# Attention with the row of maxima subtracted once per step, in quarters of the TensorE array

## The reference

```
q = einsum('bnsd,neod->bneso', sx, wq);  k = einsum(... wk);  v = einsum(... wv)
causal = where(tril(ones((s, s))), 0, -inf)
scores = einsum('bnesd,bntd->bnest', q, k) * d ** 0.5 + causal
att = softmax(scores, axis=-1)
qkv = einsum('bnest,bntd->bnesd', att, v)
```

## Time and profile before

| | us |
|---|---|
| median of 3 runs | 3643.19 (3640.71 to 3644.28) |
| profiled execution | 3640.48 |
| its span | 3638.5 |
| TensorE busy | 3115.9 (86%) |
| GpSimd busy | 1863.7 (51%) |
| VectorE busy | 1758.2 (48%) |
| ScalarE busy | 1237.5 (34%) |

### The profile page before, as it was taken

One profiled execution on the slowest core, in us unless ns is written; L12 is line 12 of the kernel. 1 busy time (PEld: TensorE's weight loads), 2 busy tenths in 40 slices (PEclk: granted clock), 3 DMA queues, 4 the chain that ended last, 5 costly groups with the idle time before them and its releaser, 6 DMA issues. The chain is left out here.

```text
span 3638.5 us, 46094 instructions
## 1 busy us (share of the span) xinstructions
PE 3115.9 (86%) x18162; PEld 1885.5 (52%) x18162; DVE 1758.2 (48%) x2797; ACT 1237.5 (34%) x1637; POOL 1863.7 (51%) x992
## 2 busy tenths in 40 slices
PE   7998654775999879899999999969899999999943
PEld 3446333554888545555555555445555555545422
DVE  4512433337774435555555564035555555564046
ACT  2200211015554223343444434423334443434423
POOL 0000000113332025677878889935677878889934
PEclk9999887687999969999999999969999999999967
DMA  9951001009998000000000000000000000000001
GB/s 393 424 172 36 0 0 51 1 8 273 273 280 151 6 14 1 1 1 1 1 1 1 1 1 1 1 1 1 1 1 1 1 1 1 1 1 1 1 4 38
DMA packets 63748, 195.36 MB, mean 54 GB/s; under 512 B 8243, under 2 KB 25137, under 8 KB 53554
## 3 DMA queue, kind: packets, MB, share of 16 engines
q1 hardware_dynamic: 38786, 148.11, 10.5%
q0 software_dynamic: 24752, 44.31, 6.8%
HBM read 188.99 MB, written 3.41 MB: 53 GB/s over the span
## 5 line engine op out<-in xcount | busy, mean ns | idle before, releaser
L1829 POOL TENSOR_TENSOR at_acc<-at_acc,at_pt 128x1024 f32<-128x1024 f32 (+3 forms) x728 | 1557.7, 2140 | 277.0 <-ACT at_pt L1665 193.7
L1725 DVE TENSOR_REDUCE at_mx<-at_psR 128x2 f32<-128x1024 f32 (+3 forms) x784 | 858.8, 1112 | 854.9 <-PE at_psR L1556 540.3
L1665 ACT ACTIVATE at_pt<-at_psR 128x1024 f32<-128x1024 f32 (+3 forms) x784 | 732.0, 936 | 993.3 <-PE at_psR L1577 601.5
L1593 PE MATMUL at_psO<-at_pt,v 128*64 128x512 f32 (+3 forms) x3136 | 706.4, 571 | 16.3 <-DVE at_oT L1744 10.6
L1574 PE MATMUL at_psR<-at_qhi,at_klo 64*128 64x512 f32 (+3 forms) x1568 | 345.5, 435 | 59.2 <-ACT at_pt L1665 28.0
L1556 PE MATMUL at_psR<-at_khi,at_qhi 64*128 64x512 f32 (+3 forms) x1568 | 340.8, 428 | 34.3 <-ACT at_pt L1665 10.2
L1593 PEld LDWEIGHTS at_psO<-at_pt,v 128*64 128x64 f32 x3136 | 193.7, 139 | 339.1 <-issue 275.2
L1209 PE MATMUL ga_acc<-h,ga_ring 128*128 128x257 f32 (+1 forms) x1352 | 307.4, 388 | 28.2 <-ACT ga_ring L1113 24.5
L1574 PEld LDWEIGHTS at_psR<-at_qhi,at_klo 64*128 64x128 f32 x1568 | 152.0, 187 | 331.1 <-issue 307.1
L1574 PE MATMUL at_psR<-at_qlo,at_khi 64*128 64x512 f32 (+3 forms) x1568 | 300.4, 376 | 0.0
L1577 PE MATMUL at_psR<-at_nm,at_ones_r 64*128 64x512 f32 (+3 forms) x1568 | 299.5, 374 | 0.0
(11 more groups left out here) (315 smaller groups left out, 3325.1 us busy)
## 6 DMA issues: line engine op xcount, KB each, us to landing
gc_rows<-in_adj SPq DMA_DIRECT2D x26, 1664.0 KB, 17.4
ga_rows<-in_adj SPq DMA_DIRECT2D x26, 1664.0 KB, 9.9
ga_ring<-in_adjT POOLq DMA_DIRECT2D x78, 512.0 KB, 24.1
gc_cols<-in_adjT SPq DMA_DIRECT2D x26, 1024.0 KB, 14.9
gc_ring<-in_adjT SPq DMA_DIRECT2D x26, 512.0 KB, 7.6
gc_ring<-in_adjT SPq DMA_DIRECT2D x13, 256.0 KB, 2.8
ga_ring<-in_adjT POOLq DMA_DIRECT2D x13, 256.0 KB, 9.9
out_x<-X SPq DMA_DIRECT2D x6, 512.0 KB
```

The source lines that it names most:

```text
L1593: ins = pe.matmul(psO[lanes[l], off:off + w], v1[:, t, (2 * hp + l) * D:(2 * hp + l + 1) * D], pt[:, g % PTS, l, 0:w], start=g == FIRST[u] ...
L1665: act.activation(pt[:, g % PTS, :, 0:w], psR[:, slot_of["score", g] % SLOTS, :, 0:w], ACT.Exp).then_inc(e_ready, 1)
L1725: dve.tensor_reduce(mx[:, u % 2, :, s, c:c + 1].rearrange("p l o -> p (l o)"), psR[:, slot_of["max", i] % SLOTS, :, 0:w], AX.X, ALU.max).t ...
L1829: pool.tensor_tensor(to, to, got, ALU.add).then_inc(added, 1)
```

## The change

The row of maxima is no longer added in `scores`, group by group. A new function `less_maxima` adds it for both groups of a step and both heads before either group's scores: four products, each in a quarter of the array (32 rows), each into a bank of its own. They now begin the accumulation (start=True), and `scores` only adds to it. For that `nm` needs the maxima in four rows, 0, 32, 64 and 96: VectorE writes each maximum twice, the transposes are 97 wide instead of 65, and `negm` has one buffer instead of two, with the wait changed to fit. `less_maxima` takes the slots of both groups; so `slot_users` lists the two score groups of a step first and all the products for maxima after them. The order in which TensorE makes these products changes a little too: the first one stands between the two groups, the others behind the second.

```diff
+QUAD = 32
 def slot_users():
             g = FIRST[u] + 2 * k
+            out += [("score", x) for x in (g + 2, g + 3) if x < FIRST[NU]]
             for half in range(2):
-                if g + 2 + half < FIRST[NU]:
-                    out.append(("score", g + 2 + half))
                 out += [("max", piece[0]) for piece in max_pieces(u, k, half)]
...
-        negm = m.sb("at_negm", [P, 2, SUB, D + 1])
+        negm = m.sb("at_negm", [P, SUB, 3 * QUAD + 1])
+        quads = [[slice((2 * l + i) * QUAD, (2 * l + i + 1) * QUAD) for l in range(2)] for i in range(2)]
...
+                def less_maxima(g):
+                    u = GROUPS[g][0]
+                    pe.wait_ge(x_read, turn_of["r", u] + 1)
+                    slots = [take_slot(pe, ("score", g + i)) for i in range(2)]
+                    for i in range(2):
+                        _, t, off, w = GROUPS[g + i]
+                        for l in range(2):
+                            pe.matmul(psR[:, slots[i], l, 0:w], ones_r[quads[i][l], :],
+                                      nm[quads[i][l], u % 2, off:off + w], start=True, stop=False)
+
                 def scores(g):
-                    pe.wait_ge(x_read, turn_of["r", u] + 1)
-                    slot = take_slot(pe, ("score", g))
+                    slot = slot_of["score", g] % SLOTS
-                    for left, right, first in ((klo, qhi, True), (khi, qlo, False), (khi, qhi, False)):
+                    for left, right, last in ((klo, qhi, False), (khi, qlo, False), (khi, qhi, True)):
                         for l in range(2):
-                            pe.matmul(psR[:, slot, l, 0:w], left[lanes[l], kc:kc + P],
-                                      right[lanes[l], u % 3, off:off + w], start=first, stop=False)
-                    for l in range(2):
-                        ins = pe.matmul(psR[:, slot, l, 0:w], ones_r[lanes[l], :], nm[lanes[l], u % 2, off:off + w],
-                                        start=False, stop=not diag)
+                            ins = pe.matmul(psR[:, slot, l, 0:w], left[lanes[l], kc:kc + P],
+                                            right[lanes[l], u % 3, off:off + w], start=False, stop=last and not diag)
...
-                        for half in range(2):
-                            if g + 2 < ng:
-                                scores(g + 2 + half)
-                            for piece in max_pieces(u, k, half):
-                                row_max(u + 2, *piece)
+                        if g + 2 < ng:
+                            less_maxima(g + 2)
+                        pieces = max_pieces(u, k, 0) + max_pieces(u, k, 1)
+                        if g + 2 < ng:
+                            scores(g + 2)
+                        for piece in pieces[:1]:
+                            row_max(u + 2, *piece)
+                        if g + 2 < ng:
+                            scores(g + 3)
+                        for piece in pieces[1:]:
+                            row_max(u + 2, *piece)
...
                 def maxima(u):
-                    if u >= 2:
-                        dve.wait_ge(x_full, turn_of["r", u - 2] + 1)
+                    if u >= 1:
+                        dve.wait_ge(x_full, turn_of["r", u - 1] + 1)
                     for s in range(bw // P):
-                        ins = dve.tensor_reduce(negm[:, u % 2, s, 0:D + 1:D], mx[:, u % 2, :, s, 0:seen], AX.X, ALU.max, negate=True)
+                        ins = dve.tensor_reduce(negm[:, s, 0:3 * QUAD + 1:QUAD].rearrange("p (l i) -> p l i", i=2),
+                                                mx[:, u % 2, :, s, 0:seen].unsqueeze(2).broadcast_to([P, 2, 2, seen]),
+                                                AX.X, ALU.max, negate=True)
```

More of the change, by code:

```diff
@@ L1528, in row_of_maxima @@
                     for s in range(QBLOCKS[UNITS[u][1]][1] // P):
-                        ins = pe.transpose(psX[0:D + 1, s * P:(s + 1) * P], negm[:, u % 2, s, :], ident[:, :])
+                        ins = pe.transpose(psX[0:3 * QUAD + 1, s * P:(s + 1) * P], negm[:, s, :], ident[:, :])
                     ins.then_inc(x_full, 1)
@@ L1608, in _ @@
                 queries(2)
+                less_maxima(0)
                 scores(0)
@@ L1644, in row_of_maxima @@
                     act.wait_ge(x_full, turn_of["r", u] + 1)
-                    act.activation(nm[0:D + 1, u % 2, 0:bw], psX[0:D + 1, 0:bw], ACT.Copy).then_inc(x_read, 1)
+                    act.activation(nm[0:3 * QUAD + 1, u % 2, 0:bw], psX[0:3 * QUAD + 1, 0:bw], ACT.Copy).then_inc(x_read, 1)
                 def turn_out(u, h):
@@ L1837, in gate @@
                             2).broadcast_to([P, ws * NE * 2, D]), ALU.mult).then_inc(weighed, 1)
-                pool.memset(negm[:, :, :, :], 0.0).then_inc(zeros, 1)
+                pool.memset(negm[:, :, :], 0.0).then_inc(zeros, 1)
                 pool.memset(nm[:, :, :].bitcast(F32), 0.0).then_inc(consts, 1)
```

## The result

| kernel | median us | against before, same chip | ratio (95%) |
|---|---|---|---|
| changed kernel | 3731.5 (3727.4 to 3735.3) | 3643.7 | 1.0242 (1.0225 to 1.0260) |
| forecast | 3736 (3668 to 3795) | | |

The change costs 88 us. The profiled execution took 3731.65 us, against 3640.48 before: 91.2 more, where the working has 93.

The account below looks back on a forecast made before the run. It took attention steps to be bound by the wait for the first score group's exponential, not TensorE's work alone. 52 + 32 + 10 + 2 + 0 − 3 = +93 us on 3640.5, plus 2.7 to the median: 3736 us (3668 to 3795).

Parts of the forecast that it names:

- A's products + 1.38 + M2 and the values: Attention step: first score group, 1.38 us through its exponential to the next-slot maxima product, then that and values (2.30): 4.71.
- Rival 3: Attention steps: TensorE's own work sets the step and the switch is free, so each loses 0.235: 3551 us; 5%.
- The 0.20 of the division: First score group's end comes 0.20 us later: 0.09 for quarters to halves plus 0.105 of exposed weight loads.
- the largest term: 260 steps with one maxima product in each half: 0.20 us longer each, +52 us.
- Rival 1: Switch between quarters and halves is free, so the 0.20 drops out everywhere: +22, 3665 us; 16%.
- Rival 2: The four quarter products run as two pairs, or their loads in line, 0.43 for 0.20: 3826 us; 14%.
- The (1,2) term: 36 steps, one then two maxima products: the third waits for the second score group's exponential, plus 0.20 each: +32 us.
- The (2,1) term: 36 steps, two then one maxima products: third 2.53 after first score group's end, before 2.38; with 0.20 each, +10 us.
- Rival 4: Three-product steps: the third maxima product's wait is hidden because ScalarE started the second group's exponential early: 3708 us; 10%.
- The 8 steps with four to six: Steps with four or six maxima products: 0.3 us longer each, +2 us.
- The −3 for GpSimd: Units whose steps have no or one maxima product: longer earlier steps leave GpSimd less behind, estimated −3 us.
- TensorE's busy time was to fall and ScalarE's to stay: Sign to look for: TensorE's product count stays, its busy time falls; ScalarE's and GpSimd's busy times stay the same.

Follow-up runs that it names:

- E7: The kernel before, with each exponential of two heads made as two activations, one per head: 3660.0 us, ratio 1.0045.
- E8: Kernel before, first maxima product moved to the step's head, except in a unit's first step and steps following a gate piece on VectorE: 3581.2 us, ratio 0.9827.
- E1: The kernel before with only the changed order of ring and steps, row of maxima still two pairs in halves behind each group's products: 3678.6 us.
- E2: The changed kernel with the row of maxima in halves of the array instead of quarters, same place and order: 3733.6 us, ratio 1.0249.
- E3: The changed kernel with the set of four products issued twice, factor 0.5 each, same sum: 3802.4 us, ratio 1.0433.
- E9: The changed kernel's quarters, with first maxima product ahead of the set and both score groups, old placing behind the gate: 3664.1 us, ratio 1.0059.
- E6: The changed kernel, but in three-product steps (not a unit's first) the first maxima product stands behind the set, ahead of both score groups: 3695.9 us.
- E4: The kernel before (halves), first maxima product moved to the step's head in all but a unit's first step: 3625.5 us, ratio 0.9951.
- E5: The changed kernel (quarters), first maxima product moved ahead of both score groups but behind the set: 3709.6 us, ratio 1.0183.

## Why the prediction was right

**The sentence that carried it held.** "The step isn't TensorE's work alone": A's products + 1.38 + M2 and the values. 1.38 is there after, to 0.01; E7 moves it by ScalarE alone, and E8 takes it out of most steps and wins 63 us. Rival 3, by which TensorE's own work sets the step, is dead on both sides.

**The 0.20 of the division held in size**, and with it the largest term (+49.8 for 52). A's end went from 1.03 to 1.24. In the 226 (1,1) steps at full clock in both timelines the step grew by 0.198 in the median and 0.18 in the mean; the other 33 give +9.4, where that mean would give 5.9: the clock's part is some 3.5. Rival 1 (the change is free, 3665 us) falls: the first pair of A stands 0.44 behind the set, not under 0.30. It would be too simple, though, to say that the change of division costs the 51 us by which the changed kernel stands above E1: E2, without that change, costs the same. The forecast had this in its sum (A's end: 0.235 off, 0.34 and 0.09 on) and did not say it as a cause.

**Rival 2** (four as two pairs, 3826 us) falls with E3. The Trainium skill, "TensorE: Matmul & The Clock Gate", Part 3, gives 3.07× for four products with K=32 and N=512; in this stream four cost 0.24, as much as a pair, so the loss it would imply isn't there. What keeps the gain away is the 0.20 at a change of division, which E9 shows for halves to quarters and back. The Trainium skill, "TensorEngine Tiling (Array Packing)", section Tiling Modes, Key Properties, says that changing the tiling mode drains the TensorE, and gives no size. The trace agrees in so far as each change costs time; a drain as such it doesn't show.

**The steps with three products: right mechanism, mis-sized.** The (1,2) term was +32 and came out as +18. It took M3 to be 1.15 behind M2 from the 2.18 of the earlier trace rows, and that row of two merged exponentials had B's lateness in it. The change itself takes B's lateness away, and 0.93 is left. E1 keeps it, and there 1.14 stands. The (2,1) term, +10, came out as +11.4: M3 is 2.48 behind A's end there (2137.84 to 2140.32) for 2.53, since the masks between A and B keep B late. Rival 4 (M3's wait hidden) falls with E1 and E6.

**The small terms, and luck.** The 8 steps with four to six were put at +2 and gave +9.3. That goes with the clock, for which the forecast had no term: the four (3,3) steps hold 51 us at half clock after and 25 before, and give +10.0, 9.2 of it in TensorE's busy time with the same products; the four (2,2) steps give −0.7. It isn't the order: E1 has them at 54.5 us, as before (54.6). In all six kernels with the row ahead of A they take 61 to 67 us and hold 40 to 60 at half clock, in the five without it 54 to 57 and 20 to 33. Which of the things that these six have in common keeps the clock down there was not tested. The −3 for GpSimd isn't seen; 51 steps with none or one gave +1.6. These two misses cancel the one of the (1,2) steps to within 3 us. That the sum is better than its terms is luck. Transposes at 97 wide cost 0.68 for four against 0.65, nothing on the whole, as counted:

```profile
2052.23 0.68 PE L1530 MATMUL at_psX<-ident,at_negm 128*97 128x128 f32 x4
```

**Wrong without consequence:** TensorE's busy time was to fall and ScalarE's to stay. TensorE's rose by 26 us, ScalarE's fell by 25. The second is the overlap of adjacent exponentials, 0.1 in most of the 260 steps. The first lies in the attention (2026.3 us in the stretch before, 2054.9 in that of after, 92 longer; by windows). Of the 27.6 us that its steps gain, 20.6 lie in the 47 steps partly at half clock, 9.2 of them in the four (3,3) steps; 6.9 lie in the 343 at full clock. Modelled ends make such a sum a weak witness of work.

## What to carry to other kernels

Before taking work off an engine, look whether the next start is set by it: in a ring of buffers, compare each start with the reader's end plus the time of its signal (0.14 us here), and count as saved only what lies on the path. Work that moves from behind a wait to ahead of it costs its full length, even if it shrinks. Here another order of the ring and of TensorE's list, by which a user waits for a reader that is long done, gave 63 us with the same instructions, while the saved products gave nothing; but check each place where that other reader is itself late (E4). And before terms are compared with a measured sum, set the steps apart in which the granted clock differs: here they hold 25 of 90 us.

## What the runs showed of the hardware

- Four products in quarters (32 rows, 512 columns, a bank each) run in the time of a pair in halves: 0.24 us for the second set of four in E3.
- A change from quarters to halves costs as much as one from halves to the values' division: the set's 0.43 to 0.44 is 0.34 + 0.09, and the first pair behind it pays 0.34 again. Together 0.20 us, nearly what the merged pair saves (0.235).
- Two exponentials of 1024 columns that follow at once take 1.94 to 1.95, where one takes 1.03: the second costs 0.92. In E9 B's products are over 0.70 after A's (last pairs at 2042.90 and 2043.60), and its exponential starts 0.92 after A's all the same.
- Cutting an exponential of 1024 columns into two of 512 lengthens M2's distance by 0.06 only.
- A product for maxima gives its slot back 1.78 us after its start (2060.96 to 2062.74): 0.55 to the reduction, 1.23 in it; its successor starts 0.14 later. So 1.92 must lie between the two: E5 has 1.73 of other products there and waits, E8 has 2.16 and E9 2.37 and don't.
- A wait of 5.7 us of TensorE is followed by half clock (E4: granted clock 0.59 in the 3.76 us from 1928.36 on). At half clock a pair of 512-column products in halves starts every 0.43 us, where it is 0.23 at full clock (E8, from 1916.27 on).
